# Node update of a four-layer graph network: the second product in fp16 halves, b3 as a column, another order of TensorE's step

## The chip, the core and the metric

The kernel runs on one NeuronCore of a Trainium2 chip (trn2). The metric is the device time of one execution in microseconds, on the core that takes it all. The engines are TensorE (PE; its weight loads are listed apart as PEld), VectorE (DVE), ScalarE (ACT), GpSimd (POOL) and SyncE (SP, which here only issues DMAs). Each engine works through its own list of instructions in order; they meet at semaphores.

## What is computed

10000 nodes with rows of 512 fp32 numbers pass through four graph layers, each with a LayerNorm and ReLU before it and a residual around it. The change is in the third layer, and there in the node update:

```python
def mish(x):
    return x * jnp.tanh(jax.nn.softplus(x))
h = mish(edge_feat @ W1 + b1)
messages = mish(h @ W2 + b2)
agg = jax.ops.segment_sum(messages, dst, num_segments=x.shape[0])
u = mish(jnp.concatenate([x, agg], axis=-1) @ W3 + b3)
out = u @ W4 + b4
y = x + out
return (y - mu) * jax.lax.rsqrt(var + LN_EPS) * gamma + beta
```

W3 and W4 have 512 columns; x here is the row after LayerNorm and ReLU. The fourth layer's LayerNorm and ReLU of the result are computed in the same phase.

## The kernel before

The kernel works on 79 tiles of 128 rows. All their activations stay in SBUF, turned (features on partitions), as two fp16 halves, high and low, with a power of two as scale (`slot_hi`, `slot_lo`). Products with such activations take three fp16 matmuls: high by high, low by high, high by low. The phases follow one another with a barrier between: `prepare` (0 to 197 us: edge lists, and the splitting of the weights into halves), the GCN layer, three SAGE layers, `edge_hidden`, `edge_messages` (to 1980), `node_update` (1980 to 2639), and the last layer with `batch_rows` and `finish` (to 3071).

`prepare` goes through the dictionary `units` of weight matrices (11 of them). For each, VectorE takes the largest absolute value (L590); from all of them together the scales `up` and `down` are formed; then ScalarE makes the high halves (`high_half`, L439) and VectorE the low ones (`low_half`, L629) in jobs of 2048 columns, one for two of the 20 tiles of edge selections and the rest behind them. The small vectors b3 and b4 become three bf16 parts each (`vec`), and three other vectors are turned into columns (`bn_cols`).

`edge_messages` works per tile of edges (20 tiles). `totals` (L1881) copies the messages' part of the W3 product, the lower half of W3, out of PSUM; `node_update` later adds it to the products of the last 20 tiles (the zone).

`node_update` (L1962) works on pairs of tiles. `by_pairs` (L1935) writes out the first six steps and the last ones and loops over the rest, two steps to a turn of the loop. In step g an engine does its stages, each with a lag in pairs; `of_pair(v, lag, stage, which)` does a stage for the tiles named of pair g − lag. Before the change the lists are:
- TensorE: `update` of pair g (for each of four chunks of features one product of b3's parts with ones, then 12 fp16 products with the 256 columns of both tiles, into `ps_z`); `second` of tile 0 of pair g−1; `turn` of both tiles of pair g−2; `second` of tile 1 of pair g−1. `second` is one product for b4, eight small ones that add the activation itself (`unscale`), and the product of `uT` with W4 in fp32, which the profile shows as eight passes (L2239). `turn` transposes the fp32 rows `h4` into `ps_t` (L222, four transposes a tile).
- ScalarE: `next_rows` of both tiles of pair g−2 (writes `h4`, L743), sigmoid, logarithm and tanh of pair g (with a load of the activation tables before each of the three), and between the last two `hi` of pair g−2 (L2195).
- VectorE: `residual` of tile 1 of pair g−2, `add_messages` of pair g (zone only), `y_stats` and `residual` of tile 0 of pair g−1, `lo` of pair g−2 (L2140), `times_z` of pair g in two instructions (L2110), `y_stats` of tile 1 of pair g−1.
- GpSimd: the LayerNorm factors (`h_factors`, `y_factor`) and `add_beta`.
- SyncE: loads and stores of the rows.

`turn` of a tile waits for `h4`, `h4` for the factors, these for `residual`, that for `y_stats`, and `y_stats` for the tile's `second`.

Of the kernel before, what the change touches and what calls it, by code (L numbers as in the profile page):

```python
# [5 lines left out]
P = 128  # L6
F32 = mybir.dt.float32
F16 = mybir.dt.float16
# [8 lines left out]
C = D // P  # L17
# [29 lines left out]
SIGMOID_FLOOR = 2.0 ** -80  # L47
PEEL = 12
# [60 lines left out]
def gnn_program(nc, x, src, dst, edge_attr, Wc, bc, Wlin, blin, Wself, Wneigh, bsage, W1, b1, W2, b2,  # L109
# [20 lines left out]
    bias_d = dram("bias_parts", [3, 2 * D], BF16)  # L130


    units = {"conv": (Wc, 1), "edge": (W1[0:2 * D, :], 2), "update": (W3[0:D, :], 1),
# [43 lines left out]
    bn_cols = sb(top, "bn_cols", [P, 3 * C])  # L177
# [41 lines left out]

    def transposes(pe, out_ap, in_ap):  # L220
# [7 lines left out]
    def prepare():  # L228
        with ExitStack() as ctx:
# [24 lines left out]
            assert jrow_at + P <= (NT - 1) * D  # L254
            VEC = 2 * D // 16
# [15 lines left out]
            bn_rows = sb(ctx, "g_bn_rows", [3 * C, P])  # L271
# [44 lines left out]
            def _(sp):  # L316
# [3 lines left out]
                for k, v in enumerate((b4, b3)):  # L320
                    sp.dma_start(vec[k * D // 16:(k + 1) * D // 16, :], v.rearrange("(p a) -> p a", a=16)).then_inc(
                        s_vec, 16)
                for k, v in enumerate((bl, gamma3, beta3)):
                    sp.dma_start(bn_rows[k * C:(k + 1) * C, :], v.rearrange("(c p) -> c p", p=P)).then_inc(s_bn, 16)
# [133 lines left out]
            def _(dve):  # L458
# [155 lines left out]
                dve.wait_ge(s_exp, 3)  # L614
                nc.vector.tensor_scalar(out=inv[:, :], in0=ex[:, :], scalar1=-1.0, scalar2=254.0,
# [24 lines left out]
                for k in range(ET // 2, len(jobs)):  # L640
                    low_half(k)

                dve.wait_ge(s_vec, 32)
                u_no = unit_no["update"]
                last_half = slice(D // 16, VEC)
                link(nc.vector.tensor_scalar(out=vec[last_half, :], in0=vec[last_half, :],
                                             scalar1=up[last_half, u_no:u_no + 1], scalar2=SCALE_LN, op0=MUL, op1=MUL))
# [17 lines left out]
                nc.vector.tensor_copy(bn_cols[:, :], ps_line[:, P:P + 3 * C])  # L665

            @block.tensor
            def _(pe):
# [32 lines left out]
                pe.wait_ge(s_bn, 48)  # L701
                nc.tensor.transpose(ps_line[:, P:P + 3 * C], bn_rows[:, :], ident[0:3 * C, 0:3 * C]).then_inc(s_bnT, 1)
# [1096 lines left out]
    def edge_messages():  # L1799
        with ExitStack() as ctx:  # L1800
# [12 lines left out]
            s_w, s_f, s_mm, s_r, s_sum, s_aT, s_mm3, s_tot = sems("n", "w f mm r sum aT mm3 tot")  # L1813
# [41 lines left out]
            def _(dve):  # L1855
# [27 lines left out]
                pipeline(dve, ET, (0, z_sum), (0, cap), (0, lambda v: mish.poly(dve, v)), (1, add), (3, totals),  # L1883
                         (0, lambda v: mish.result(dve, r[:, :], v)), peel=8)
# [77 lines left out]
    def node_update():  # L1962
        with ExitStack() as ctx:
            w3 = sb(ctx, "u_w3", [P, 2 * cols["update"]], F16)
            w4 = sb(ctx, "u_w4", [P, C * D])
            gam, bet = (sb(ctx, f"u_{n}", [P, D]) for n in ("gam", "bet"))
            b3_rows = sb(ctx, "u_b3_rows", [3, D], BF16)
            b4_rows = sb(ctx, "u_b4_rows", [3, D], BF16)
            ones3 = sb(ctx, "u_ones3", [3, 2 * P], BF16)
            f = sb(ctx, "u_f", [P, 1])  # L1970
            minus_f = sb(ctx, "u_minus_f", [P, 1])
            unscale = sb(ctx, "u_unscale", [P, P], F16)
            uT = [sb(ctx, f"u_uT{b}", [P, C * 2 * P]) for b in range(2)]
# [6 lines left out]
            (s_w, s_f, s_w4, s_ones, s_mm, s_added, s_s, s_l, s_th, s_u, s_mm4, s_yn, s_xb, s_ry, s_x3, s_h4,  # L1980
             s_turn, s_hi, s_lo) = sems(
                "u", "w f w4 ones mm added s l th u mm4 yn xb ry x3 h4 turn hi lo")
# [3 lines left out]
            u_no = unit_no["update"]  # L1986
            block = ctx.enter_context(nc.Block())

            def ut_tile(v, c):
                return uT[v.j // 2][:, c * 2 * P + (v.j % 2) * P:c * 2 * P + (v.j % 2 + 1) * P]  # L1990
# [13 lines left out]
            def _(sp):  # L2004
                sp.dma_start(w3[:, :], split_d["update"][:, :]).then_inc(s_w, 16)
                sp.dma_start(b3_rows[:, :], bias_d[:, D:2 * D]).then_inc(s_w, 16)
                sp.dma_start(b4_rows[:, :], bias_d[:, 0:D]).then_inc(s_w, 16)
                sp.dma_start(w4[:, :].rearrange("p (c n) -> p c n", c=C),
                             W4.rearrange("(c p) n -> p c n", p=P)).then_inc(s_w, 16)
# [38 lines left out]
            def _(pool):  # L2048
                nc.gpsimd.memset(ones3[:, :], 1.0).then_inc(s_ones, 1)
                pool.wait_ge(s_w, 96)  # L2050
# [7 lines left out]
                def y_factor(v):  # L2058
                    b = v.buf(2)
                    pool.wait_ge(normy.s_mv, v.t + 1)  # L2060
                    nc.gpsimd.tensor_tensor(out=normy.ve[b][:, :], in0=normy.mv[b][:, 1:2], in1=eps_col[:, :],
# [18 lines left out]
            def _(dve):  # L2080
                nc.vector.tensor_scalar(out=f[:, :], in0=down[:, u_no:u_no + 1], scalar1=1.0 / SCALE_LN,
                                        scalar2=None, op0=MUL).then_inc(s_f, 1)
                nc.vector.tensor_scalar(out=minus_f[:, :], in0=down[:, u_no:u_no + 1], scalar1=-1.0 / SCALE_LN,
                                        scalar2=None, op0=MUL).then_inc(s_f, 1)
                dve.wait_ge(s_f, 2)
                dve.wait_ge(s_w, 96)
# [69 lines left out]
            def _(act):  # L2156
# [13 lines left out]
                def z_there(v, k):  # L2170
                    act.wait_ge(s_mm, mish_count(v, k))
                    if k == 0:
                        wait_count(act, s_mm4, v.t - 2)
# [331 lines left out]
```

## Time and profile before

| | |
|---|---|
| Median of three timed runs | 3079.21 us (3074.42 to 3087.73) |
| The profiled execution, whole | 3073.27 us |
| Its span, first to last instruction | 3071.0 us |
| Mean granted TensorE clock | 0.950 |
| PE, DVE, ACT, POOL busy | 84%, 60%, 49%, 40% of the span |
| Table loads of ScalarE at L2167 | 120 |

Times in the profile are microseconds from the start of the span. "Busy" counts the instructions of an engine. The granted clock is TensorE's share of full speed; it has two levels, 1.2 and 2.4 GHz, so that a stretch at 0.5 ran at the lower. Matmuls follow each other faster than one lasts: the distance from one start to the next is what a matmul costs.

### The profile page before, as it was taken

How to read it: one execution, taken by the hardware profiler on the slowest of the kernel's cores; microseconds unless marked ns; L12 is line 12 of the kernel's file. 1: busy time of each engine (PE TensorE's matmuls, PEld its weight loads, DVE VectorE, ACT ScalarE, POOL GpSimd, SP SyncE). 2: the span in 40 equal slices, each digit the busy share in tenths (PEclk: the TensorE clock that was granted, in tenths of full speed). 3: DMA queues.
4: the chain of work that ended last, by engine and by line, in shares of the span. 5: the costliest groups of instructions: out<-in, count | busy, mean ns of one | idle time of the engine just before them, and what ended most of it. 6: DMA issues, size and time to landing. Idle time of an engine off the chain costs nothing. (4 is left out here: it accounts for less than half of the span.)

```text
span 3071.0 us, 44367 instructions
## 1 busy us (share of the span) xinstructions
PE 2573.3 (84%) x13170; PEld 1453.0 (47%) x13170; DVE 1851.7 (60%) x4344; ACT 1505.4 (49%) x2128; POOL 1221.5 (40%) x2065
## 2 busy tenths in 40 slices
PE   0347888789887999798979969799999999899964
PEld 0234554344443445344544547565555555444443
DVE  8744876578666876799864435345555566423333
ACT  7235665345333533355335756466666666332270
POOL 3666874236332332365545511133333333100146
PEclk9999998899998999899989989899999999999976
DMA  5154442278766887666553322322222234101268
GB/s 173 59 213 124 150 145 92 78 184 201 134 123 156 203 171 152 192 221 220 181 182 105 101 80 85 103 81 95 96 99 102 89 134 138 71 1 38 57 225 312
DMA packets 379160, 412.03 MB, mean 134 GB/s; under 512 B 198351, under 2 KB 237683, under 8 KB 376316
## 3 DMA queue, kind: packets, MB, share of 16 engines
q1 hardware_dynamic: 350364, 335.34, 37.0%
q0 software_dynamic: 28640, 74.78, 8.1%
q8 instruction: 78, 1.28, 0.2%
q14 instruction: 78, 0.64, 0.1%
HBM read 171.50 MB, written 197.28 MB: 120 GB/s over the span
## 5 line engine op out<-in xcount | busy, mean ns | idle before, releaser
L215 PE MATMUL s_ps_z<-s_w,slots 128*128 128x512 f16 x2844 | 645.7, 384 | 41.7 <-DMA s_bias<-in_L_gnn_b 41.7
L215 PEld LDWEIGHTS s_ps_z<-s_w,slots 128*128 128x128 f16 (+1 forms) x2844 | 280.9, 99 | 363.3 <-DMA s_bias<-in_L_gnn_b 43.1
L1571 ACT ACTIVATE s_g<-s_g,s_rn 128x512 f32<-128x512 f32 x237 | 170.0, 717 | 287.7 <-POOL s_rn L1461 287.7
L2239 PE MATMUL u_ps_o<-u_w,u_uT 128*128 128x512 f32 x632 | 288.6, 599 | 0.2 <-DVE u_uT L2110 0.2
L1461 POOL TENSOR_TENSOR s_rn<-s_em,minus_half 128x1 f32<-128x1 f32 x237 | 179.6, 758 | 253.0 <-DVE s_em L1515 245.1
L1500 DVE SCALAR_TENSOR_TENSOR s_g<-s_ps_z,s_f,s_bias 128x512 f32<-128x512 f32 x237 | 177.9, 751 | 140.3 <-PE s_ps_z L215 132.0
L2221 PE MATMUL u_ps_z<-slots,u_w 128*128 (+2 forms) x1920 | 236.7, 273 | 0.0
L2349 PE MATMUL z_ps_z<-slots,z_w 128*128 128x512 f16 (+1 forms) x960 | 211.7, 380 | 7.2 <-DMA z_w<-split_root 7.2
L2221 PEld LDWEIGHTS u_ps_z<-slots,u_w 128*128 128x128 f16 x1920 | 173.9, 98 | 37.7 <-issue 0.4
L716 DVE BATCH_NORM_STATS2 u_ny_st<-u_ps_o 128x6 f32<-128x512 f32 x79 | 54.7, 692 | 213.7 <-PE u_ps_o L2239 213.7
L743 ACT ACTIVATE u_h<-u_x,u_n_sh,u_n_rs 128x512 f32<-128x512 f32 x79 | 64.3, 814 | 229.3 <-POOL u_n_sh L738 229.3
L2239 PEld LDWEIGHTS u_ps_o<-u_w,u_uT 128*128 128x128 f32 x632 | 113.9, 190 | 113.7 <-issue 113.3
L1508 DVE SCALAR_TENSOR_TENSOR s_junk<-s_g 128x512 f32<-128x512 f32 x237 | 164.5, 694 | 4.1
L2167 ACT ACT_TABLE_LOAD x120 | 154.0, 1283 | 26.3 <-PE u_ps_z L2221 24.1
L215 PE MATMUL s_ps_z<-s_wn,s_aT 128*128 128x512 f16 x720 | 165.2, 379 | 0.0
L2318 DVE BATCH_NORM_STATS2 z_stats<-slots 128x6 f32<-128x512 f32 (+1 forms) x76 | 52.2, 687 | 185.7 <-ACT slots L2335 185.7
L743 ACT ACTIVATE s_h<-s_x,s_norm_sh,s_norm_rs 128x512 f32<-128x512 f32 x79 | 64.2, 813 | 176.0 <-POOL s_norm_sh L738 95.9
L2349 PEld LDWEIGHTS z_ps_z<-slots,z_w 128*128 128x128 f16 x960 | 94.6, 99 | 116.0 <-DMA z_w<-split_root 7.6
L2335 ACT ACTIVATE slots<-z_ps_z,bn_cols,z_f 128x512 f32<-128x512 f32 (+1 forms) x76 | 58.7, 772 | 158.3 <-PE z_ps_z L2349 158.2
L1292 POOL DMA_INDIRECT z_m<-h_rows,src_s x20 | 19.0, 950 | 257.1 <-DVE z_aT L1338 251.7
L215 PEld LDWEIGHTS s_ps_z<-s_wn,s_aT 128*128 128x128 f16 x720 | 70.4, 98 | 85.0
L1526 DVE SCALAR_TENSOR_TENSOR s_halves<-s_g,s_halves 128x512 f16<-128x512 f32 x158 | 108.0, 684 | 2.5 <-ACT s_halves L1559 2.5
(370 smaller groups left out, 5445.0 us busy)
## 6 DMA issues: line engine op xcount, KB each, us to landing
h_rows<-s_g SPq DMA_DIRECT2D x158, 256.0 KB
x_rows<-q_x SPq DMA_DIRECT2D x79, 256.0 KB
s_x<-x_rows SPq DMA_DIRECT2D x79, 256.0 KB
x_rows<-s_x SPq DMA_DIRECT2D x79, 256.0 KB
h_rows<-s_h SPq DMA_DIRECT2D x79, 256.0 KB
u_x<-x_rows SPq DMA_DIRECT2D x79, 256.0 KB
x_rows<-u_x SPq DMA_DIRECT2D x79, 256.0 KB
h_rows<-u_h SPq DMA_DIRECT2D x79, 256.0 KB
```

Source lines behind the costliest of these rows:

```text
L215: ins = nc.tensor.matmul(out_ap, a(c), w[:, part * size + c * n:part * size + (c + 1) * n], start=first and c == 0 and m == 0, stop=stop a ...
L743: return nc.scalar.activation(out_ap, in_ap, func, scale=self.rstd[b][:, 0:1], bias=self.shift[b][:, 0:1])
L1461: nc.gpsimd.tensor_tensor(out=rn[b][:, :], in0=em[b][:, :], in1=minus_half[:, :], op=POW).then_inc(s_rn, 1)
L1500: nc.vector.scalar_tensor_tensor(out=g[b][:, :], in0=ps_z[v.buf(4)][:, :], scalar=f[:, 0:1], in1=bias[:, :], op0=MUL, op1=ADD).then_inc(s_ ...
L1508: nc.vector.scalar_tensor_tensor(out=junk[:, :], in0=r[:, :], scalar=0.0, in1=r[:, :], op0=MAX, op1=MUL, accum_out=en[e][:, 0:1]).then_inc ...
L1526: nc.vector.scalar_tensor_tensor(out=part[:, D:2 * D], in0=g[v.buf(ng)][:, :], scalar=scale_out, in1=part[:, 0:D], op0=MUL, op1=SUB).then_ ...
L1571: nc.scalar.activation(g[b][:, :], g[b][:, :], ACT.Relu, scale=rn[v.buf(2)][:, 0:1]).then_inc(s_h, 1)
L2167: nc.scalar.activation(part, z if first else part, func, scale=scale, **kw).then_inc(sem, 1)
L2221: ins = nc.tensor.matmul(z, w3[:, at:at + P], pair_slots[:, :, part * D + k * P:part * D + (k + 1) * P], start=False, stop=k == C - 1 and ...
L2239: ins = nc.tensor.matmul(ps_o[b][:, :], ut_tile(v, c), w4[:, c * D:(c + 1) * D], start=False, stop=c == C - 1)
L2335: nc.scalar.activation(z_of(zx, g, c)[:, 0:n], ps_z[c][:, 0:n], ACT.Identity, scale=f[:, 0:1], bias=bn_cols[:, c:c + 1]).then_inc(s_z, 1)
L2349: ins = nc.tensor.matmul(out_ap, weights[:, at:at + P], a(k), start=first and k == 0 and m == 0, stop=stop and k == C - 1 and m == 2)
```

## The change

W4 becomes a further unit of `prepare` and is kept as fp16 halves. In `node_update` the product `u` is also split into halves, `u_hi` by ScalarE (`hi_u`, a copy with a scale) and `u_lo` by VectorE (`lo_u`), and `second` multiplies halves: high by both halves of W4, then low by the high half, 12 fp16 matmuls of 512 columns. The scale `g` of `u` is found on the chip from the largest value that z can have: `edge_messages` takes the largest absolute value of each tile of message products (`z_max`), and a chain of some twenty small VectorE instructions with one product of TensorE at the start of `node_update` makes `g` and the scales that follow from it (`k_h`, `k_b`, `eps_y`). b3 is no longer a product: it is a column, added as the bias of the sigmoid and in `times_z`, so both now work on one chunk of features at a time, four instructions of 256 columns each in place of two of 512. The table load before the tanh is written out and names a set that also has the sigmoid. `uT`, `u_hi` and `u_lo` have one buffer each; `uT` had two. TensorE's step is now `update`, both `turn`, both `second`. In `edge_messages` VectorE's list is written out for all tiles instead of a loop.

```diff
@@ prepare
-    units = {"conv": (Wc, 1), "edge": (W1[0:2 * D, :], 2), "update": (W3[0:D, :], 1),
+    units = {"conv": (Wc, 1), "edge": (W1[0:2 * D, :], 2), "update": (W3[0:D, :], 1), "out": (W4, 1),
-                for k, v in enumerate((bl, gamma3, beta3)):
+                for k, v in enumerate((bl, gamma3, beta3, b3)):
+                two = slice(unit_no["update"], unit_no["out"] + 1)
+                link(nc.vector.tensor_scalar(out=ex[:, two], in0=ex[:, two], scalar1=157.0, scalar2=None, op0=MIN))
@@ edge_messages, VectorE
+                    wait_count(dve, s_zmax, v.t - 1)
                     nc.vector.tensor_scalar(out=tot[b][:, :], in0=ps_g[b][:, :], scalar1=scale[:, 0:1],
                                             scalar2=None, op0=MUL).then_inc(s_tot, 1)
+                    dve.wait_ge(s_tot, v.t + 1)
+                    nc.vector.tensor_reduce(out=z_max[:, v.t:v.t + 1], in_=tot[b][:, :], op=MAX, axis=AX.X,
+                                            apply_absolute_value=True).then_inc(s_zmax, 1)
@@ node_update, VectorE
-                        nc.vector.tensor_tensor(out=part, in0=z, in1=part, op=MUL).then_inc(s_u, 1)
+                def times_z(v, tiles):
+                    for c in range(C):
+                        dve.wait_ge(s_th, mish_count(v, c // 2))
+                        part = chunk(uT, c, tiles)
+                        ins = nc.vector.scalar_tensor_tensor(out=part, in0=z_chunk(v, c, tiles), scalar=b3_cols[:, c:c + 1],
+                                                             in1=part, op0=ADD, op1=MUL)
+                        if c % 2:
+                            ins.then_inc(s_u, 1)
+                def lo_u(k):
                     def stage(v, tiles):
+                        dve.wait_ge(s_uhi, mish_count(v, k))
+                        nc.vector.scalar_tensor_tensor(out=half(u_lo, k, tiles), in0=half(uT, k, tiles), scalar=g[:, 0:1],
+                                                       in1=half(u_hi, k, tiles), op0=MUL, op1=SUB).then_inc(s_ulo, 1)
...
-                    whole_pair(v, 0, times_z(0))
-                    whole_pair(v, 0, times_z(1))
+                    whole_pair(v, 0, times_z)
+                    whole_pair(v, 0, lo_u(0))
+                    whole_pair(v, 0, lo_u(1))
                     of_pair(v, 1, y_stats, (1,))
@@ node_update, ScalarE
+                def sigmoid(v, tiles):
+                    for c in range(C):
+                        z_there(v, c // 2)
+                        if c % 2 == 0:
+                            wait_count(act, s_ulo, mish_count(v, c // 2) - 2)
+                        ins = nc.scalar.activation(chunk(uT, c, tiles), z_chunk(v, c, tiles), ACT.Sigmoid,
+                                                   scale=minus_f[:, 0:1], bias=minus_b3[:, c:c + 1])
...
+                def tanh(v, tiles):
+                    load_sigmoid_and_tanh(act)
...
+                def hi_u(v, tiles):
+                    wait_count(act, s_mm4, v.t)
+                    for k in range(2):
+                        act.wait_ge(s_u, mish_count(v, k))
+                        nc.scalar.activation(half(u_hi, k, tiles), half(uT, k, tiles), ACT.Copy,
+                                             scale=g[:, 0:1]).then_inc(s_uhi, 1)
...
                     whole_pair(v, 0, tanh)
+                    whole_pair(v, 0, hi_u)
@@ node_update, TensorE
-                        nc.tensor.matmul(z, b3_rows[:, c * P:(c + 1) * P], ones3[:, 0:tiles * P], start=True, stop=False)
...
-                    pe.wait_ge(s_u, 2 * v.g + 2)
+                    pe.wait_ge(s_uhi, 2 * v.g + 2)
+                    for part in range(2):
+                        for c in range(C):
+                            nc.tensor.matmul(ps_o[b][:, :], chunk_of_tile(u_hi, v, c),
+                                             w4[:, part * cols["out"] + c * D:part * cols["out"] + (c + 1) * D],
+                                             start=False, stop=False)
+                    pe.wait_ge(s_ulo, 2 * v.g + 2)
                     for c in range(C):
-                        ins = nc.tensor.matmul(ps_o[b][:, :], ut_tile(v, c), w4[:, c * D:(c + 1) * D],
+                        ins = nc.tensor.matmul(ps_o[b][:, :], chunk_of_tile(u_lo, v, c), w4[:, c * D:(c + 1) * D],
                                                start=False, stop=c == C - 1)
...
                 def step(v):
                     whole_pair(v, 0, update)
+                    of_pair(v, 2, turn)
                     of_pair(v, 1, second, (0,))
-                    of_pair(v, 2, turn)
                     of_pair(v, 1, second, (1,))
```

## Rows read from the trace of the kernel before

**Rows 1.** Busy time by stretch: start:end, us, then PE, PEld, DVE, ACT, POOL, clock, DMA.
```profile
2006.00:2610.00 604.00, 604.00 (x3512) 357.04 (x3512) 344.70 (x788) 384.10 (x490) 225.68 (x524) 1.00 0.30 106
```

**Rows 2.** Timeline of TensorE, one step: start, us, engine, line, operation, count, idle before.
```profile
2207.84 0.28 PE L2217 MATMUL u_ps_z<-u_ones,u_b_rows 3*128 3x256 bf16 x1
2208.05 1.48 PE L2221 MATMUL u_ps_z<-slots,u_w 128*128 x12
...
2214.35 0.39 PE L2230 MATMUL u_ps_o<-u_b_rows,u_ones 3*128 3x512 bf16 x1
...
2215.12 3.65 PE L2239 MATMUL u_ps_o<-u_w,u_uT 128*128 128x512 f32 x8
2218.61 1.04 PE L222 MATMUL u_ps_t<-ident,u_h 128*128 128x128 f32 x8
2219.58 0.39 PE L2230 MATMUL u_ps_o<-u_b_rows,u_ones 3*128 3x512 bf16 x1
...
2223.94 0.28 PE L2217 MATMUL u_ps_z<-u_ones,u_b_rows 3*128 3x256 bf16 x1
```

**Rows 3.** Timeline of VectorE in the same step.
```profile
2218.82 0.70 DVE L716 BATCH_NORM_STATS2 u_ny_st<-u_ps_o 128x6 f32<-128x512 f32 x1 [6.22 <-PE u_ps_o L2239]
...
2222.67 1.29 DVE L2140 SCALAR_TENSOR_TENSOR slots<-u_ps_t,slots 128x512 f32 x2
2223.87 1.28 DVE L2110 TENSOR_TENSOR u_uT<-u_ps_z,u_uT 128x512 f32<-128x512 f32 x2
2225.07 0.69 DVE L716 BATCH_NORM_STATS2 u_ny_st<-u_ps_o 128x6 f32<-128x512 f32 x1
```

**Rows 4.** Timeline of ScalarE in the same step.
```profile
2217.34 1.28 ACT L2167 ACT_TABLE_LOAD   x1
2218.64 1.33 ACT L2167 ACTIVATE u_uT<-u_uT,floor_col 128x512 f32<-128x512 f32 x2
...
2222.25 1.15 ACT L2167 ACTIVATE u_uT<-u_uT 128x512 f32<-128x512 f32 x2
...
2230.01 0.81 ACT L743 ACTIVATE u_h<-u_x,u_n_sh,u_n_rs 128x512 f32<-128x512 f32 x1 [5.16 <-POOL u_n_sh L738]
```

**Rows 5.** Groups by shape of the node update: busy us and mean ns, idle before.
```profile
L2126 DVE SCALAR_TENSOR_TENSOR u_ps_o<-u_ps_o,u_ny_mv,u_gam 128x512 f32<-128x512 f32 x79 | 59.9, 759 | 4.7 <-DVE u_ny_mv L2121 2.3
L2110 DVE TENSOR_TENSOR u_uT<-u_ps_z,u_uT 128x512 f32<-128x512 f32 x78 | 49.8, 678 | 12.6 <-ACT u_uT L2167 12.6
L2101 DVE TENSOR_TENSOR u_ps_z<-u_ps_z,u_zg 128x256 f32<-128x256 f32 x40 | 15.2, 422 | 17.0 <-PE u_ps_z L2221 17.0
L2167 ACT ACTIVATE u_uT<-u_ps_z,u_minus_f 128x512 f32<-128x512 f32 x77 | 48.7, 683 | 1.7 <-PE u_ps_z L2221 1.2
L2167 ACT ACTIVATE u_uT<-u_ps_z,u_minus_f 128x256 f32<-128x256 f32 x2 | 0.8, 470 | 0.0
```

**Rows 6.** Stretches around TensorE's pauses (columns of rows 1), and turns at the phase's end.
```profile
2631.10:2635.50 4.40, 0.00 (x0) 0.00 (x0) 2.79 (x6) 1.41 (x2) 1.50 (x5) 0.80 0.31 119
2643.80:2647.80 4.00, 3.95 (x11) 1.46 (x12) 0.00 (x0) 0.00 (x0) 0.00 (x0) 0.55 0.76 309
2647.80:2658.00 10.20, 10.20 (x49) 4.65 (x48) 2.55 (x8) 3.11 (x4) 0.00 (x0) 1.00 0.05 13
1990.80:1995.80 5.00, 4.96 (x24) 3.12 (x25) 1.42 (x2) 0.00 (x0) 3.07 (x2) 0.54 0.26 100
...
2630.44 0.66 PE L222 MATMUL u_ps_t<-ident,u_h 128*128 128x128 f32 x4 [1.54 <-ACT u_h L743]
2635.53 1.12 PE L222 MATMUL u_ps_t<-ident,u_h 128*128 128x128 f32 x4 [4.43 <-ACT u_h L743]
```

**Rows 7.** Groups by shape of the preparation.
```profile
L629 DVE SCALAR_TENSOR_TENSOR w_parts<-slots,up,w_parts 128x2048 f16<-128x2048 f32 x11 | 25.8, 2351 | 3.7 <-ACT w_parts L439 3.7
L590 DVE TENSOR_REDUCE w_mx<-slots 128x1 f32<-128x2048 f32 x9 | 19.8, 2279 | 0.0
```

**Rows 8.** Timeline of VectorE, one tile of the message phase.
```profile
1870.17 0.69 DVE L1865 TENSOR_TENSOR n_r<-n_ps,n_bias 128x512 f32<-128x512 f32 x1 [0.84 <-PE n_ps L1906]
```

More of the change, by code:

```diff
@@ L176, in gnn_program @@
         sb(top, n, [P, ET]) for n in ("zone_slot", "home", "dis_dst", "carry_c"))
-    bn_cols = sb(top, "bn_cols", [P, 3 * C])
+    bn_cols = sb(top, "bn_cols", [P, 4 * C])
+    z_max = sb(top, "z_max", [P, ET + C])
     up = sb(top, "up", [P, NU])
@@ L641, in _ @@
                     low_half(k)
[L643 to L647, printed above, removed]
+                dve.wait_ge(s_vec, 16)
                 for m in range(3):
@@ L1985, in node_update, with chunk_of_tile, half, chunk @@
             normy, norm3 = Norm(ctx, "u_ny", 2), Norm(ctx, "u_n3", 2)
-            u_no = unit_no["update"]
+            u_no, o_no = unit_no["update"], unit_no["out"]
             block = ctx.enter_context(nc.Block())
-            def ut_tile(v, c):
-                return uT[v.j // 2][:, c * 2 * P + (v.j % 2) * P:c * 2 * P + (v.j % 2 + 1) * P]
+            def chunk_of_tile(buf, v, c):
+                return buf[:, c * 2 * P + (v.j % 2) * P:c * 2 * P + (v.j % 2 + 1) * P]
+            def half(buf, k, tiles):
+                return buf[:, k * D:(k + 1) * D].rearrange("p (c n) -> p c n", c=2)[:, :, 0:tiles * P]
+            def chunk(buf, c, tiles):
+                return buf[:, c * 2 * P:c * 2 * P + tiles * P]
+            def z_chunk(v, c, tiles):
+                return ps_z[v.j // 2][c // 2][:, (c % 2) * 2 * P:(c % 2) * 2 * P + tiles * P]
             def mish_count(v, k):
@@ L2156, in _ @@
             def _(act):
-                act.wait_ge(s_f, 2)
-                def each_half(sem, before, func, scale, bias=None, first=False):
-                    def stage(v, tiles):
-                        b = v.j // 2
-                        for k in range(2):
-                            before(v, k)
-                            part = uT[b][:, k * D:(k + 1) * D].rearrange("p (c n) -> p c n", c=2)[:, :, 0:tiles * P]
-                            z = ps_z[b][k][:, :].rearrange("p (c n) -> p c n", c=2)[:, :, 0:tiles * P]
-                            kw = {} if bias is None else {"bias": bias}
-                            nc.scalar.activation(part, z if first else part, func, scale=scale, **kw).then_inc(sem, 1)
-                    return stage
+                act.wait_ge(s_f, 1)
@@ L2182, in _ @@
-                sigmoid = each_half(s_s, z_there, ACT.Sigmoid, minus_f[:, 0:1], first=True)
-                log = each_half(s_l, s_there, ACT.Ln, 1.0, bias=floor_col[:, 0:1])
-                tanh = each_half(s_th, l_there, ACT.Tanh, -1.0)
+                def sigmoid(v, tiles):
[5 more added lines that the diff above has]
+                                                   scale=minus_f[:, 0:1], bias=minus_b3[:, c:c + 1])
+                        if c % 2:
+                            ins.then_inc(s_s, 1)
@@ new lines, in log @@
+                def log(v, tiles):
+                    for k in range(2):
+                        act.wait_ge(s_s, mish_count(v, k))
+                        nc.scalar.activation(half(uT, k, tiles), half(uT, k, tiles), ACT.Ln, scale=1.0,
+                                             bias=floor_col[:, 0:1]).then_inc(s_l, 1)
+                def tanh(v, tiles):
+                    load_sigmoid_and_tanh(act)
+                    for k in range(2):
+                        act.wait_ge(s_l, mish_count(v, k))
+                        nc.scalar.activation(half(uT, k, tiles), half(uT, k, tiles), ACT.Tanh, scale=-1.0).then_inc(s_th, 1)
@@ L2215, in update @@
                     for c in range(C):
[L2216 to L2217 removed]
+                        z = z_chunk(v, c, tiles)
                         for k in range(C):
```

134 lines of the change are left out of this document (81 added, 53 removed).

## The prediction

> **What bounds the kernel now.** I read the stages first. The whole change lives in the node update, apart from one more weight matrix in the preparation and one small reduction per tile of the message phase. In the steady part of the node update TensorE is busy for 604.00 of 604.00 us at full granted clock, while VectorE is busy for 344.70 and ScalarE for 384.10 [rows 1]. So in this stage TensorE is the bound, and the question is what bounds it once TensorE has less to do.
>
> Next I read one step of TensorE. A step is one pair of tiles; it runs from the bias product at 2207.84 to the same product at 2223.94, which is 16.10 us [rows 2]. In it stand: update 2207.84 to 2214.35, 6.51; second product of tile 0 to 2218.61, 4.26; both turns to 2219.58, 0.97; second product of tile 1 to 2223.94, 4.36. No wait stands between them. The phase lasts from 1990.8 to about 2638, which is 40 such steps.
>
> Then I read VectorE in the same step. It sits idle for 6.22 us until the second product of tile 0 is done, and then works through in program order: y_stats and residual of tile 0, both `lo`, both `times_z`, y_stats and residual of tile 1 [rows 3]. It is late only because TensorE is late. The last tile's factors come from GpSimd and let ScalarE write the new rows `h4` at 2230.01 [rows 4]. The turn reads these rows. Before the change a whole second product stands between the update and that turn, so the turn finds them ready.
>
> **The change, part by part.**
>
> TensorE's work. (a) The four b3 products go: 2208.05 − 2207.84 = 0.21 each, 0.84 a step [rows 2], which leaves 5.67 for the update. (b) Of a second product, b4 and the unscale products stay: 2214.35 to 2215.12, 0.77. The eight fp32 passes, 2215.12 to 2218.61, 3.49, become 12 fp16 products of 512 columns. The last stage has such products: 49 in 10.20 us, 0.21 each, so 12 take 2.59 at the usual 0.216 [rows 6]. A second product takes 3.36. (c) With the turns at 0.97 and some 0.1 at the loop's edge the step's work is 5.67 + 0.97 + 6.72 + 0.1 = 13.5 us, 2.6 less than now.
>
> The order. Now `turn` of the pair g−2 stands ahead of `second` of tile 0 of pair g−1. That closes a ring which was open. Followed from the start of y_stats of tile 0:
> - y_stats, residual, both `lo`: 2218.82 to 2223.87, 5.05 us [rows 3].
> - `times_z` and the new `lo_u`. Now `times_z` takes 2223.87 to 2225.07, 1.20. It becomes four instructions of 256 columns with a per-partition scalar: a 512-wide one with such a scalar takes 759 ns, 256 columns less save 678 − 422 = 256 ns, and successive ones overlap by some 80 ns, so 0.42 each, 1.68 [rows 5]. The two `lo_u` are like `lo`, two in 1.29 less the overlap, plus the scalar: 0.66 each, 1.32. Together 3.0 us, 1.8 more. ScalarE's `hi_u` stands between, but it starts when half of `times_z` is done and takes about 0.6, so the first `lo_u` finds it nearly ready. For these instructions I take 2.7 to 3.3 as bounds.
> - y_stats and residual of tile 1, GpSimd's four small instructions, ScalarE's `h4`: 2225.07 to 2230.82, 5.75 us [rows 3, 4].
> - TensorE, from `h4` on: a wake-up of about 0.1, the turn of that tile 0.49, the second product of tile 0 3.36, and about 0.22 until VectorE sees it: 4.17 us.
>
> The sum is 5.05 + 3.0 + 5.75 + 4.17 = 18.0 us. It is a ring, since that second product releases the next y_stats. It doesn't matter that TensorE needs only 13.5: it would stand still for 4.5 us in each step, between the turns of the first and of the second tile. At full clock the step is 18.0 − 16.1 = 1.9 us longer, over 40 steps +76.
>
> The clock. TensorE then idles for about 4.5 us in one piece. The trace has one such place, at the end of the same phase: 4.40 us with no matmul, the granted clock falls to 0.80 of full within it, and the four transposes behind it take 1.12 us where eight took 1.04 in the steady step [rows 2, 6]. So the level of 1.2 GHz was in force where 2.4 had been. After a longer pause the clock stays at about 0.55 for 4.96 us (start of the node update) or 3.95 us (start of the last stage) of dense matmuls before it is back at full [rows 6]. At half rate half the work is done, so the loss is 2.0 to 2.5 us. The first work behind the gap is the turn and the second product of tile 0, 3.85 us of it, and all of it is on the ring. Bounds are 0 and 3.85; I take 2.3, the middle of the two rows. The step becomes 20.3 us, +4.2, over 40 steps +168. The rest of TensorE's step (5.67 + 3.36 + 0.49 = 9.5 us) fits beside the other 13.8 us of the ring, so the gap stays and the clock falls anew in each step.
>
> ScalarE. One table load of 1.28 goes; the sigmoid becomes four of 256 columns with scalar and bias columns: 470 ns for one with the scalar alone, some 0.1 more for the bias (`h4` has both at 512 columns and takes 0.81 against 683 ns), less the overlap, 0.47 each, 1.9 [rows 4, 5]; `hi_u` adds 1.2. From `h4` at the ring to the first half of tanh: 1.9 + 1.28 + (2218.64 to 2222.25) 3.61 + 0.6 = 7.4 us [rows 4]. VectorE reaches `times_z` 4.17 + 5.05 = 9.2 us after `h4`. So ScalarE has 1.8 us to spare, the table load saved is worth nothing, and if all three loads stayed (1.28 more) that would still cost nothing.
> On what a load costs the trace and a page differ. The load at 2217.34 ends at 2218.62 and the logarithm starts at 2218.64 [rows 4]: 1.28 us, all told. The Trainium skill, "ScalarE: Activation LUTs", section "What ACT_TABLE_LOAD costs", adds about 1.38 us of drain to each switch; by that ScalarE's branch would be 10.2 us here, 1.0 more than its cover at full clock, 40 us in all, and still covered if the clock halves. The row decides: no drain is seen.
>
> Preparation. W4 becomes a twelfth unit with one more piece of 2048 columns: one more absolute maximum of 2.28 us ahead of all scales, and one more low half of 2.35 us at the end of VectorE's list, which leads up to the store of the selections that the phase ends with [rows 7]. +4.6 us, none of it covered; bounds 2 and 6.
>
> Messages. `z_max` adds about 0.7 us of VectorE per tile (a 512-wide instruction) between the copy of the sums and the next `mish` result. VectorE waits 0.84 us for TensorE once per tile [rows 8], which covers it: 0, at worst 20 × 0.7 = 14 if that cover were gone.
>
> Start of the node update. Some twenty chained VectorE instructions of 0.2 us run while the weights load or while the first products run; TensorE gets one small product more: 0.3 us, bounds 0 and 2.
>
> Sum: 168 + 4.6 + 0.3 = +173 on the profiled execution's 3073.3, of which 3071.0 is the span: 3246. The median of the three timed runs is 3079.2, 6 above it: **3252**, predicted as 3250.
>
> **The rivals.**
> (A) The ring holds but the clock stays at full, because the turn of the first tile in the gap, or the dense rest of the step, keeps it up. Then +76 + 5: 3160. Against it: the gap of 4.40 us above also had a turn just ahead of it, at 2630.44 [rows 6].
> (B) TensorE stays the bound, and the change does what TensorE's sums say: 40 × −2.6 = −104, +5: 2980, faster. This needs the rows `h4` of the second tile before update and first turn are over, which is 9.5 us after the second product of tile 0 (second product of tile 1, update, turn); the other engines need 13.8 for it. It decides at the point where these two are equal; 4.3 us would have to go, so a step of the program order that I misread.
> (C) The ring is about 2 us shorter than I sum it (256-wide instructions cheaper, `lo_u` out of the way), TensorE's gap is then 2.5 us and the clock mostly stays: no change, 3085.
> (D) The half clock feeds itself: TensorE never gets the clock back, its 13.5 us become 27 and it is the bound again: 40 × 10.9, about 3515. Against it: in the last stage and at the start of this one dense matmuls brought the clock back within 5 us [rows 6].
>
> **How the numbers follow.** Ring with the clock falling 0.67; (A) 0.16; (B) 0.08; (C) 0.03; (D) 0.06. The forecast's own spread is 2.0 to 3.85 us of clock loss and 17.7 to 18.3 of ring: 3225 to 3310. The range goes down to (A) and up to the top of that spread: 3145 to 3305. A measurement of this kernel can tell 0.5% (15 us) from no change: faster 0.08 (B), within 0.03 (C), slower 0.89.
>
> **What would show it.** In the profile after: TensorE in the node update with some 38 waits of 4 to 5 us at `u_ps_t` for ScalarE's `u_h`, a granted clock near 0.85 instead of 1.00 in the steady part, a step of 20 us from update to update, transposes of the second tile at 1.1 us per four; VectorE idle 6 to 9 us before y_stats of tile 0 and nowhere else; two table loads a step; the last stage starting 170 us later, after a message phase as long as before. If TensorE's wait at the turn is under 2 us, the ring is misread. If the wait is 4.5 and the clock 1.00, (A) holds and the clock's term is wrong. If ScalarE's tanh is what `times_z` waits for, its branch is longer than I make it.

## The result, and the profile after

The changed kernel takes 3266.08 us (median of four, 3260.41 to 3269.34) against 3076.82 beside it: ratio 1.061 [1.058, 1.063], slower by 6.1%, which is 189 us between the medians. 3250 was forecast. The brackets behind a ratio are its 95% interval.

The page of the kernel after; the first line of digits under it is the granted TensorE clock in 40 slices, the second the share of the DMA engines:
```profile
span 3267.6 us, 45171 instructions
...
PE 2562.0 (78%) x13328; PEld 1468.7 (45%) x13328; DVE 1943.4 (59%) x4543; ACT 1533.1 (47%) x2250; POOL 1217.4 (37%) x2065
...
PEclk9999998899989998999899898888888888799976
DMA  5154442388658876665532222222222233200258
```
The run of eights from the 25th to the 35th slice is the node update; there the clock was at full before. Busy time by stretch (columns as in [rows 1]), first a long piece of the node update, then one gap of TensorE, the work behind it, and the rest of the step:
```profile
2011.00:2600.00 589.00, 451.94 (x2863) 285.88 (x2862) 306.29 (x684) 318.99 (x471) 171.28 (x395) 0.84 0.22 76
2319.40:2324.40 5.00, 0.00 (x0) 0.00 (x0) 2.38 (x5) 0.85 (x2) 2.69 (x7) 0.80 0.28 105
2324.40:2330.80 6.40, 6.38 (x26) 3.11 (x26) 0.00 (x0) 6.35 (x10) 1.56 (x2) 0.62 0.38 123
2330.80:2339.80 9.00, 9.00 (x73) 6.72 (x73) 8.28 (x19) 3.59 (x6) 1.81 (x6) 1.00 0.08 29
```
TensorE is busy for 452 of 589 us where it was busy without a break in [rows 1], and no engine is the bound: each waits for another. The waits of the node update name the circle (who waits, for whom, total us, times, longest):
```profile
POOL u_ny_ve L2081 <- DVE u_ny_mv L2185: 406.3, 79, 14.5
DVE u_ny_st L719 <- PE u_ps_o L2318: 330.6, 40, 9.1
PE u_ps_t L228 <- ACT u_h L746: 196.3, 42, 5.8
ACT u_hi L2255 <- DVE u_uT L2165: 177.1, 40, 5.7
```
One step in the timeline of the kernel after, all engines, which answers to [rows 2 to 4]:
```profile
2310.29 0.70 DVE L719 BATCH_NORM_STATS2 u_ny_st<-u_ps_o 128x6 f32<-128x512 f32 x1 [8.66 <-PE u_ps_o L2318]
...
2315.35 1.65 DVE L2165 SCALAR_TENSOR_TENSOR u_uT<-u_ps_z,u_b_cols,u_uT 128x256 f32<-128x256 f32 x4
...
2317.07 1.47 DVE L2173 SCALAR_TENSOR_TENSOR u_lo<-u_uT,u_g,u_hi 128x512 f16<-128x512 f32 x2
...
2318.46 0.69 DVE L719 BATCH_NORM_STATS2 u_ny_st<-u_ps_o 128x6 f32<-128x512 f32 x1
...
2318.79 0.60 PE L228 MATMUL u_ps_t<-ident,u_h 128*128 128x128 f32 x4
...
2323.55 0.81 ACT L746 ACTIVATE u_h<-u_x,u_n_sh,u_n_rs 128x512 f32<-128x512 f32 x1 [5.09 <-POOL u_n_sh L741]
...
2324.42 1.11 PE L228 MATMUL u_ps_t<-ident,u_h 128*128 128x128 f32 x4 [5.03 <-ACT u_h L746]
...
2326.83 3.09 PE L2313 MATMUL u_ps_o<-u_w,u_hi 128*128 128x512 f16 x8
2329.76 1.03 PE L2318 MATMUL u_ps_o<-u_w,u_lo 128*128 128x512 f16 x4
2330.82 0.70 DVE L719 BATCH_NORM_STATS2 u_ny_st<-u_ps_o 128x6 f32<-128x512 f32 x1 [8.61 <-PE u_ps_o L2318]
2331.49 1.89 PE L2313 MATMUL u_ps_o<-u_w,u_hi 128*128 128x512 f16 x8
```
The ring of the prediction can be read off: y_stats of tile 0 at 2310.29, times_z at 2315.35 (5.06 later), y_stats of tile 1 at 2318.46 (3.11), h4 ended at 2324.36 (5.90), y_stats of the next tile 0 at 2330.82 (6.46). The step is 20.53 us. The same four transposes take 1.11 us behind the gap and 0.60 ahead of it, the same eight products 3.09 and 1.89.

Where the span's +197 us lie: the last stage started at 2639.0 and now at 2828.9; the node update itself went from 658.8 to 832.5, +173.7. The preparation gave +11.8, the stages from GCN to the edges +4, the messages +0.2, the last stage +7.

### The profile page after: what moved, and what is told of

The parts are those of the page before. It is cut to its first block and busy times, and to the rows that moved or that the text cites. A ratio compares the mean times of both kernels' runs of the same rounds, so it can differ in the third digit from the quotient of the medians.

```text
span 3267.6 us, 45171 instructions
## 1 busy us (share of the span) xinstructions
PE 2562.0 (78%) x13328; PEld 1468.7 (45%) x13328; DVE 1943.4 (59%) x4543; ACT 1533.1 (47%) x2250; POOL 1217.4 (37%) x2065
## 5 line engine op out<-in xcount | busy, mean ns | idle before, releaser
L228 PE MATMUL u_ps_t<-ident,u_h 128*128 128x128 f32 x316 | 68.1, 355 | 196.3 <-ACT u_h L746 196.3
L2294 PE MATMUL u_ps_z<-slots,u_w 128*128 (+2 forms) x1920 | 215.9, 273 | 0.0
L2313 PE MATMUL u_ps_o<-u_w,u_hi 128*128 128x512 f16 x632 | 202.8, 478 | 2.0 <-ACT u_hi L2255 2.0
L2294 PEld LDWEIGHTS u_ps_z<-slots,u_w 128*128 128x128 f16 x1920 | 187.3, 99 | 30.5
L2081 POOL TENSOR_TENSOR u_ny_ve<-u_ny_mv,u_eps_y 128x1 f32<-128x1 f32 x79 | 15.0, 190 | 406.3 <-DVE u_ny_mv L2185 406.3
L2255 ACT ACTIVATE u_hi<-u_uT,u_g 128x512 f16<-128x512 f32 (+1 forms) x80 | 57.3, 717 | 177.3 <-DVE u_uT L2165 177.1
L228 PEld LDWEIGHTS u_ps_t<-ident,u_h 128*128 128x128 f32 x316 | 46.8, 179 | 207.3 <-ACT u_h L746 206.9
```

The source lines that it names most:

```text
L2255: nc.scalar.activation(half(u_hi, k, tiles), half(uT, k, tiles), ACT.Copy, scale=g[:, 0:1]).then_inc(s_uhi, 1)
L2294: ins = nc.tensor.matmul(z, w3[:, at:at + P], pair_slots[:, :, part * D + k * P:part * D + (k + 1) * P], start=k == 0 and m == 0, stop=k = ...
L2313: nc.tensor.matmul(ps_o[b][:, :], chunk_of_tile(u_hi, v, c), w4[:, part * cols["out"] + c * D:part * cols["out"] + (c + 1) * D], start=Fal ...
```

## The experiments

The kernels of the first eight experiments ran beside a kernel before of 3062 to 3063 us, the last four beside one of 3078, so ratios are compared. A mean step is the mean of the 37 steps from TensorE's third update to its last; "the loop's steps" are those that `by_pairs` doesn't write out.

**The turn alone moved back** (e1).
```diff
                     whole_pair(v, 0, update)
-                    of_pair(v, 2, turn)
                     of_pair(v, 1, second, (0,))
+                    of_pair(v, 2, turn)
                     of_pair(v, 1, second, (1,))
```


> The changed kernel with one line moved: TensorE turns the rows after the second product of tile 0 again, as in the kernel before; halves, b3 column and two table loads stay. My theory (the closed ring costs the time, the halves don't): the second product of tile 0 leaves the ring. The next ring is VectorE and ScalarE: times_z and lo_u 3.1, y_stats of tile 1 to the end of h4 5.9, sigmoid to the first half of tanh 7.4, with wake-ups 16.6 us a step instead of 20.5. TensorE's work of 13.5 falls in several smaller gaps, so the clock comes back: 3266 - 3.9 x 40 = 3110 us (3090 to 3130), the granted clock of the steady part above 0.95, TensorE's waits for u_h gone. Rival 1 (the added vector and scalar instructions and the small chunks are what costs, wherever TensorE turns): the step stays above 18.5 and the time above 3180. Rival 2 (TensorE's own 13.5 us decide once the turn is back): 3266 - 7 x 40 = 2985.

Measured: 3073.91, ratio 1.004 [1.003, 1.006]. With one line moved the kernel is 12 us slower than the one before instead of 189, with all the new instructions in place. Its step is 16.3 us, by ScalarE's rows of this kernel, which stand in VectorE's and ScalarE's ring now:
```profile
2316.30 0.81 ACT L746 ACTIVATE u_h<-u_x,u_n_sh,u_n_rs 128x512 f32<-128x512 f32 x1 [5.09 <-POOL u_n_sh L741]
...
2332.57 0.81 ACT L746 ACTIVATE u_h<-u_x,u_n_sh,u_n_rs 128x512 f32<-128x512 f32 x1 [4.93 <-POOL u_n_sh L741]
```
Three things of the expectation failed. The step is 16.3 us and not 16.6, which puts the time at the lower edge of what was expected. The waits at the turn are fewer but not gone (74.4 us in 33 waits up to 2640). And the clock isn't back everywhere: its mean is 0.93 in 2011 to 2600, and behind one gap of 3.17 us eight products took 2.91 us. That costs nothing: from one h4 of tile 0 to the next it is 16.27 to 16.45 us in every step of the steady part, whether the clock falls in it or not, while TensorE's own steps vary from 13.2 to 19.5. TensorE is not in this ring.

**Only the turn moved, in the kernel before** (e2): the same line, the other way, with fp32 W4.

> The kernel before with nothing but the turn moved ahead of both second products: fp32 W4, one times_z of 512 columns a half, three table loads. My theory: the ring closes here too, 5.05 + 1.2 + 5.75 + (0.1 + 0.49 + 4.26 + 0.22) = 17.1 us against 16.1 of TensorE's work, so a step of 17.1 with gaps of only 1.0 us, which leave the clock at full: 3077 + 40 = 3117 us (3100 to 3130). If even this gap lets the clock fall: 3077 + 3.3 x 40 = 3210. Rival (the order does harm only with the halves, or not at all): 3077, within 5.

Measured: 3108.94, ratio 1.016 [1.014, 1.017], +47. The loop's steps take 17.1, and the granted clock stays at 1.00 (columns as in [rows 1]):
```profile
2011.00:2600.00 589.00, 566.44 (x3257) 329.33 (x3256) 317.51 (x722) 352.96 (x451) 208.28 (x484) 1.00 0.28 98
```
So the order alone closes the ring, without halves. TensorE's pause in it is 0.8 us here and 5.0 in the changed kernel, which has less work for TensorE and a longer ring.

**A third table load, in the changed kernel (e3) and with the turn moved back (e4).**
```diff
                 def sigmoid(v, tiles):
+                    load_sigmoid_and_tanh(act)
                     for c in range(C):
```


> The changed kernel with a third table load a step put back ahead of the sigmoids. My theory: ScalarE reaches tanh 1.8 us before VectorE asks for it, so 1.28 more is covered: 3266, within 6. Rival (ScalarE's branch is on the ring, or each switch costs more than the 1.28 shown): +1.28 x 40 = +51 or more, 3317.

> The first kernel (turn back behind the second product of tile 0) with the third table load. If the next ring is the one I name, with ScalarE's sigmoid to tanh in it, the load is on the path in full now: +1.28 x 39 = +50 over the first kernel, about 3160. If the first kernel is bound by anything else (TensorE, or VectorE alone): within 8 of it.

Measured: e3 1.061 [1.059, 1.062], the same as the changed kernel; e4 3135.95, ratio 1.024 [1.023, 1.026], +62 over e1, where +50 was expected. The same instruction is free in one ring and costs in full in the other. In e4 ScalarE's h4 of tile 0 comes every 17.71 us instead of 16.27, so a load costs 1.44: its 1.28, and 0.16 more. Most of the 0.16 is overlap lost between its neighbours: the sigmoids start 2.13 us after h4 does, against 0.73 in e1, which is 1.28 + 0.12.
```profile
2313.77 0.81 ACT L746 ACTIVATE u_h<-u_x,u_n_sh,u_n_rs 128x512 f32<-128x512 f32 x1 [5.09 <-POOL u_n_sh L741]
2314.60 1.28 ACT L223 ACT_TABLE_LOAD   x1
2315.90 1.93 ACT L2235 ACTIVATE u_uT<-u_ps_z,u_minus_b,u_minus_f 128x256 f32<-128x256 f32 x4
```
The Trainium skill, "ScalarE: Activation LUTs", section "What ACT_TABLE_LOAD costs", would have it at 1.28 + 1.38; the measurement decides, and no such drain is in it.

**The gap filled, with 14 products (e5) and with 20 (e12).** In the changed kernel's own order TensorE gets work that nobody uses, between the two turns.
```diff
                 def turn(v):
-                    pe.wait_ge(s_h4, v.t + 1)
                     wait_count(pe, s_lo, v.t - 1)
+                    if v.j % 2:
+                        for k in range(14):
+                            nc.tensor.matmul(ps_t[v.buf(2)][:, :], w4[:, 0:P], w4[:, 0:D], start=True, stop=True)
+                    pe.wait_ge(s_h4, v.t + 1)
```


> The changed kernel in its own order, with 14 fp16 products of 512 columns (0.216 us each, 3.0 in all) put on TensorE between the turns of the first and of the second tile, into the bank that the second turn then overwrites: they compute nothing that is used and fill 3.0 of the 5.0 us in which TensorE stood still. My theory: the clock's term is real and apart from the ring's. With the gap filled the clock stays at full, four transposes of the second tile take 0.60 instead of 1.11 us, and the step is the bare ring, 18.3 us instead of 20.5: 2.2 x 40 = 88 us less than the changed kernel, so about 100 above the kernel before (ratio 1.032). Rival (the slow products behind the gap have another cause, or extra products in the gap only delay the turn): no gain, ratio 1.061 or above.

> The changed kernel in its own order with 20 filler products (4.3 us) instead of 14 between the two turns. With 14, steps of 17.76 us, in which the clock held, alternated with steps of 19.4 to 20.0, in which it fell in spite of them: 18.8 in the mean. With 20 TensorE stands still for about 0.6 us only. If the clock's fall is what makes the long steps, all become 17.8: 1.0 x 39 = 39 less than with 14, ratio 1.026 (1.022 to 1.030). If the long steps have another cause: ratio 1.039. If the filler itself becomes the bound: above 1.039.

Measured: e5 1.039 [1.038, 1.041], e12 1.030 [1.029, 1.032]. More work on TensorE makes the kernel faster, by 3% of its time. The stretch 2100 to 2500 of the changed kernel, of e5 and of e12 (columns as in [rows 1]):
```profile
2100.00:2500.00 400.00, 306.26 (x1923) 192.43 (x1923) 209.12 (x467) 211.12 (x313) 116.82 (x272) 0.83 0.22 77
2100.00:2500.00 400.00, 359.84 (x2318) 217.63 (x2318) 221.30 (x494) 225.18 (x334) 125.86 (x290) 0.94 0.24 82
2100.00:2500.00 400.00, 386.36 (x2597) 236.77 (x2595) 236.31 (x528) 237.59 (x352) 133.55 (x308) 1.00 0.25 87
```
With 14 a pause of up to 2.0 us is left, and steps of 17.75 to 18.29 alternate with ones of 19.44 to 19.97 (mean 18.86). So not all of the clock's loss came back, and 1.039 missed the 1.032 that was expected. With 20 the clock holds and the mean step is 18.0 (18.13 to 18.31 in the loop, 17.77 in the steps written out). The turn behind the filled gap in e12:
```profile
2303.96 0.66 PE L228 MATMUL u_ps_t<-ident,u_h 128*128 128x128 f32 x4 [0.56 <-ACT u_h L746]
2304.55 0.38 PE L2304 MATMUL u_ps_o<-u_b_rows,u_ones 3*128 3x512 bf16 x1
```
So the bare ring is 18.0 us in the mean, and the clock's part is the mean of the changed kernel, 20.4, less that: 2.4 a step.

**VectorE's order** (e6, with the changed kernel's TensorE order; e7, with the turn moved back too; e8, e7 with the third load).
```diff
-                    of_pair(v, 2, residual, (1,))
                     of_pair(v, 0, add_messages(0))
                     of_pair(v, 0, add_messages(1))
                     of_pair(v, 1, y_stats, (0,))
                     of_pair(v, 1, residual, (0,))
                     of_pair(v, 2, lo)
+                    of_pair(v, 1, y_stats, (1,))
                     whole_pair(v, 0, times_z)
+                    of_pair(v, 1, residual, (1,))
                     whole_pair(v, 0, lo_u(0))
                     whole_pair(v, 0, lo_u(1))
-                    of_pair(v, 1, y_stats, (1,))
```


> The changed kernel with TensorE's order left alone and VectorE's step changed: y_stats of tile 1 goes ahead of times_z, and the residual of tile 1 follows right behind times_z, ahead of both lo_u. My theory of one ring: the two lo_u (1.5) leave it, and half a microsecond of y_stats goes elsewhere: ring 16.4 to 16.6 us at full clock, TensorE's gap 3.0 to 3.5, still with a fallen clock behind it (2.3): step 18.7, 1.8 x 40 = 72 less than the changed kernel, ratio about 1.037. If the clock holds in the shorter gap: ratio 1.007. Rival (VectorE's order is no part of the ring): ratio 1.061.

> Both orders changed: TensorE turns behind the second product of tile 0 (as in the first kernel), VectorE does y_stats of tile 1 ahead of times_z and its residual ahead of both lo_u. The ring that bound the first kernel at 16.4 us loses both lo_u and y_stats: times_z 1.7, residual 2.5, GpSimd 1.3, h4 0.8, sigmoid to the first half of tanh 7.4, wake-ups 0.3: 14.0 us, against 13.5 of TensorE's work. So the step is 13.8 to 14.0, the time 2.5 x 40 = 100 below the first kernel: ratio to the kernel before 0.972 (0.968 to 0.980), the fp16 halves pay at last. Rival (GpSimd's add_beta in front of the factors, or x rows loaded too late, takes the place): step 15.4 to 16.4, ratio 0.99 to 1.004.

> The kernel with both orders changed, plus the third table load. Theory: ScalarE's branch is in its ring, so 1.28 to 1.5 us a step comes back: ratio 0.988 to 0.992, 50 to 60 us above the kernel without it. If TensorE were the bound there instead: within 10 us of it.

Measured: e6 1.052 [1.050, 1.054], expected 1.037; e7 3009.66, 0.983 [0.981, 0.985], expected 0.972; e8 3065.68, 1.001 [1.000, 1.002], 56 above e7 as expected. The order of e7 is 1.7% faster than the kernel before, and with the third load put back (e8) nothing of that is left. The step of e7 is 14.56, not 14.0. Its timeline says why:
```profile
2311.41 1.38 DVE L2173 SCALAR_TENSOR_TENSOR u_lo<-u_uT,u_g,u_hi 128x512 f16<-128x512 f32 x2
2311.57 0.61 POOL L733 TENSOR_TENSOR u_n_nm<-u_n_mv,minus_one 128x1 f32<-128x1 f32 x1 [3.33 <-DVE u_n_mv L727]
2312.14 0.71 POOL L734 TENSOR_TENSOR u_n_ve<-u_n_mv,eps_col 128x1 f32<-128x1 f32 x1
```
These two GpSimd instructions take 0.19 us each in the changed kernel. Here they are in the ring and stand beside lo_u: 0.94 us more.

In e6 the same happens, and a second thing. Its mean step is 19.9, forecast 18.7, and most of the loop's steps take 20.48, as long as the changed kernel's. Two of its rows of VectorE and three stretches, which answer to those of the changed kernel above:
```profile
2310.87 0.70 DVE L719 BATCH_NORM_STATS2 u_ny_st<-u_ps_o 128x6 f32<-128x512 f32 x1 [9.20 <-PE u_ps_o L2318]
...
2331.35 0.70 DVE L719 BATCH_NORM_STATS2 u_ny_st<-u_ps_o 128x6 f32<-128x512 f32 x1 [9.20 <-PE u_ps_o L2318]
...
2320.60:2324.00 3.40, 0.03 (x1) 0.00 (x1) 1.51 (x5) 0.87 (x2) 2.91 (x5) 0.99 0.42 154
2324.00:2331.40 7.40, 7.40 (x26) 3.38 (x26) 0.05 (x1) 7.34 (x12) 1.54 (x2) 0.54 0.32 106
2331.40:2340.50 9.10, 8.61 (x69) 6.23 (x68) 8.40 (x20) 2.59 (x4) 2.54 (x8) 1.00 0.08 29
```
From y_stats of tile 0 to the end of h4 (2323.94) it is 13.07 us, 1.0 less than the changed kernel's 14.07, where 1.8 was expected: GpSimd's two instructions cost 0.9 here too. But from there to the next y_stats it is 7.41 instead of 6.46, and the order of that work is the same. What differs is where the low clock lies. The pause of 5.0 us in the changed kernel had a granted clock of 0.80, so a part of the slow time was spent on nothing; the pause of 3.4 us here has 0.99, and the work behind it 0.54 instead of 0.62. So the clock took back what was left of the gain. It had been priced at the same 2.3 us.

**What slows GpSimd there** (e10): e7 with lo_u reading z from PSUM. This leaves the low half of u, and so the second product, other than the reference's.
```diff
-                        nc.vector.scalar_tensor_tensor(out=half(u_lo, k, tiles), in0=half(uT, k, tiles), scalar=g[:, 0:1],
+                        nc.vector.scalar_tensor_tensor(out=half(u_lo, k, tiles), in0=half(ps_z[v.j // 2][k], 0, tiles), scalar=g[:, 0:1],
...
-                    wait_count(pe, s_u, 2 * v.g - 2)
+                    wait_count(pe, s_ulo, 2 * v.g - 2)
```


> The kernel with both orders in which the two lo_u read their first operand from z in PSUM instead of from uT in SBUF (same instruction, shape and place; what they compute is not the low half, so the second product is not the reference's). TensorE's update waits for them instead of for times_z, which was long done. Theory: lo_u slows GpSimd because both its tensor operands lie in SBUF, as the Trainium skill, SBUF - State Buffer, states for GpSimd instructions that read SBUF. Then nm and ve of tile 1 (0.61 and 0.71 us) go back to 0.19 each, the step from 14.56 to 13.6 or 13.7, ratio 0.970 to 0.973. Rival 1 (any VectorE instruction of that length does it, or the fp16 output): 0.61 and 0.71 stay, ratio 0.983. Rival 2 (these GpSimd instructions are long but off the ring): they shorten and the time stays at 0.983.

Measured: ratio 0.976 [0.974, 0.978]. Groups of 2100 to 2500 of this kernel:
```profile
L733 POOL TENSOR_TENSOR u_n_nm<-u_n_mv,minus_one 128x1 f32<-128x1 f32 x59 | 11.2, 190 | 154.5 <-DVE u_n_mv L727 154.5
L734 POOL TENSOR_TENSOR u_n_ve<-u_n_mv,eps_col 128x1 f32<-128x1 f32 x59 | 11.2, 189 | 0.0
```
190 and 189 ns again, with the same length and fp16 output of lo_u: the second operand in SBUF was the cause. The step came out as forecast, 13.6; the ratio is above its range by some 8 us, and about 6 of these lie ahead of the node update, in the preparation (below).

**Tile work first** (e9), and the same orders in the kernel before (e11).
```diff
-                    of_pair(v, 2, residual, (1,))
                     of_pair(v, 0, add_messages(0))
                     of_pair(v, 0, add_messages(1))
                     of_pair(v, 1, y_stats, (0,))
                     of_pair(v, 1, residual, (0,))
+                    of_pair(v, 1, y_stats, (1,))
+                    of_pair(v, 1, residual, (1,))
+                    whole_pair(v, 0, times_z)
                     of_pair(v, 2, lo)
-                    whole_pair(v, 0, times_z)
                     whole_pair(v, 0, lo_u(0))
                     whole_pair(v, 0, lo_u(1))
-                    of_pair(v, 1, y_stats, (1,))
...
-                    of_pair(v, 2, turn)
                     of_pair(v, 1, second, (0,))
                     of_pair(v, 1, second, (1,))
+                    of_pair(v, 2, turn)
```


> The changed kernel with both orders changed further: VectorE does y_stats and residual of both tiles before times_z, then lo and the two lo_u; TensorE turns behind both second products. In the kernel with both orders, of 14.56 us a step, GpSimd's two first factor instructions of tile 1 took 0.61 and 0.71 us instead of 0.19 and stood beside lo_u, which I hold to be the cause of 0.95 us of its ring. Here those factors run beside times_z, which reads one operand from PSUM, so they take 0.19 again, and the ring (VectorE's tile work, factors, h4, sigmoid to tanh, times_z) is shorter than TensorE's own 13.5 us: TensorE is the bound at last, step 13.4 to 13.6, 1.0 x 39 = 40 us less than with both orders, ratio to the kernel before 0.966 to 0.973, TensorE without a wait of over 0.5 us. Rival (something else holds the step at 14.5, GpSimd's add_beta or the late x rows): ratio 0.98 or above.

> The kernel before, fp32 W4 and three table loads, with the orders of the tile-first kernel: VectorE y_stats and residual of both tiles, times_z, lo; TensorE turns last. Theory: TensorE was the bound at 16.1 us without a wait, so no order gives anything: ratio 1.000 within 0.003. Then what the tile-first kernel gains is from the halves, set free by the order. Rival (the order alone is worth it): ratio below 0.99.

Measured: e9 3005.35, ratio 0.977 [0.975, 0.979], the fastest that computes the reference; e11 1.001 [0.999, 1.002], its step 16.10 as before. So the order alone gives nothing, and with the parts of the change (halves, b3 as a column, one table load fewer) it gives 2.3%. Which of the parts it is wasn't separated in this order; in e7's the table load saved was worth all of the gain (e8). e9 fell short of its range: the mean step is 13.74, not 13.5, and TensorE still waits for lo_u, because the collision has changed sides. GpSimd's add_beta starts first now, and it is VectorE that stands still:
```profile
2314.32 2.51 POOL L2075 TENSOR_TENSOR u_x<-u_x,u_bet 128x512 f32<-128x512 f32 x2
...
2315.78 1.60 DVE L2173 SCALAR_TENSOR_TENSOR u_lo<-u_uT,u_g,u_hi 128x512 f16<-128x512 f32 x1
```
One of the two lo_u takes 1.60 us where it takes 0.75 alone. A version with add_beta out of lo_u's way wasn't tried.

## Why the prediction was right

**The ring.** Forecast 5.05 + 3.0 + 5.75 + 4.17 = 18.0; measured 5.06, 3.11 and 5.90 in the trace of the changed kernel, and TensorE's part with the clock held 4.21 (e12, from the end of h4 at 2303.91 to y_stats at 2308.12). That is 18.3, and the loop's steps of e12 take 18.13 to 18.31. That the order closes it, and not the added work, is shown by e1 and e2. Two small terms were short: from y_stats of tile 1 to h4 it took 0.15 more, and times_z with lo_u 0.1 more. The mean of e12 is 18.0 all the same, because the steps written out take 17.77.

**The clock.** Forecast 2.3 from [rows 6], at most 3.85; 2.4 by e12. TensorE's part of the ring took 6.46 against 4.17 + 2.3. That the clock would fall in each step, and cost work in the ring, was right. That its price met 2.3 so closely is in part luck: the price isn't a constant, as the prediction took it. It is 3.2 in e6 (7.41 less 4.21), behind a pause that is shorter by 1.6 us. And the step is a weak test of the ring's length: by estimate the bare ring is 17.3 us in e6's loop (13.07 + 4.21), 18.2 in the changed kernel's loop and 17.8 in its steps written out (both from e12), and yet all three mostly take 20.4 to 20.5 with the clock falling. It is e12 that tests the 18.0. Rival (A), full clock, is out: its time would have been about e12's. That the gap's turn of the first tile doesn't keep the clock up was read rightly from the one gap of 4.40 us. Rival (D) is out as well: in the step shown the clock is back at full from 2330.8 on, 6.4 us behind the gap, and the next gap finds it there.

**ScalarE.** That a third load would cost nothing came out so (e3). In the step shown the first half of tanh ends at about 2331.7 and times_z starts at 2335.88: 4.2 us of cover, which is the 1.8 forecast and the clock's 2.3. The cover was that of this ring alone. In both other orders tried with it a load costs some 1.44 (17.71 less 16.27, 15.99 less 14.56), so the table load saved is worth about 56 us in e7, as much as e7 gains on the kernel before; the prediction, which priced it at nothing, was right only for the kernel at hand.

**Messages.** z_max takes 0.69 us a tile and the stage is as long as before, +0.2 in all.

**Preparation, the term that was too small in the profile of after.** Forecast +4.6; there it is +11.8, while e1 and e3 to e8, with the same preparation, hand over at 203.1 to 203.6 (GCN's first product) against 198.95 in e2, which has the old one: +4.1 to +4.7. Run on another chip, e9, e10 and e12 hand over at 207.6, 209.6 and 212.8, and e11, with the old one, at 199.1. So the term is right for the work, and 4 to 9 us more come in some executions. In the profile of after a part of them shows in TensorE's waits for g_selT in the loop over the selections (20.8 us in all, up to 6.6 each; before 17.4, up to 3.6). What VectorE and ScalarE stand still for there isn't settled.

**TensorE's sum.** 13.5 was forecast; in e9 the update takes 5.33 (from 2309.54 to 2314.87) instead of 5.67, both turns 0.88 instead of 0.97, and the second product 3.36 as forecast: 12.9 without waits. It mattered to no number here, but it is what rival (B) needed: with e9's order the step falls to 13.74 and the kernel to 0.977. (B) said 2.6 less a step and 2980, a ratio of 0.968. e9 gives 2.4 less and stays some 30 us above that. (B)'s claim was wrong for this order.

**The range.** The top of the forecast's spread was added up wrongly: 40 × (18.3 + 3.85 − 16.1) is 242, which gives 3326 and not 3310. It changes nothing at 3266.

Against the profiled execution, 3269.3, the sum of 3246 is 23 us short: 5 in the node update, 7 in the preparation, 4 in the stages up to the edges and 7 in the last one, in which nothing was changed.

## What to carry to other kernels

When the bounding engine gets less to do, ask what waits for it and what it waits for, and follow that circle once round: if a turn of it is longer than the engine's new work, the circle is the time. Moving one consumer ahead of an unrelated piece of work can put that piece into the circle; moving one back can take it out, and here one line was worth some 174 us. Price a saved instruction anew for each order, since the same table load was worth nothing in one and 56 us in another. And price a pause of TensorE by the work behind it that runs at the low clock, not by a fixed sum.

## What the hardware showed that was not expected

- VectorE's lo_u, with two operands in SBUF, and GpSimd's instructions that read SBUF don't run side by side: 0.61 and 0.71 us instead of 0.19 for GpSimd's (e7), 0.19 again with one operand in PSUM (e10), and 1.60 instead of 0.75 for VectorE's where GpSimd had started first (e9). The Trainium skill, "SBUF — State Buffer", section "Who interferes with whom", says so: a VectorE instruction with two inputs in SBUF contends with a GpSimd instruction that reads SBUF, for a port pair that is locked exclusively, and the order of issue decides who waits. Both directions are seen here. I hadn't applied it to e6 and e7.
- The clock fell behind pauses well under the 4.4 us of [rows 6] too: in e1 a pause of 3.17 us, with the granted clock at 0.70 in the 5.6 us behind it, and in some of e5's steps, where no pause of the loop is above 2.03. In e7 and e9, whose pauses in the loop are under 1 us, it stayed at 1.00.
- A shorter pause can cost more: 3.4 us in e6 cost the ring 3.2 us, 5.0 us in the changed kernel 2.3, because the clock was still at 0.99 in the one and at 0.80 in the other, and the slow stretch then fell on the work.
- Work that nobody uses, put into a pause of TensorE, made the kernel 3% faster, because the work behind the pause was in the ring and the pause was not TensorE's to give.
